# Token rounds of a two-layer Flamingo kernel: router logits computed transposed, routing sums kept in PSUM, one wait for the four quantised tiles

## The reference, cut to what matters

```python
x = x + tanh(g_xattn[0]) * _L0_xattn_ref(ctx, _layernorm(x), conv_w, conv_b, ...)   # adds layernorm(x) and a small convolution
x = x + tanh(g_ffn[0])   * _L0_ffn_ref(_layernorm(x), weight, bias)                 # see below
x = x + tanh(g_xattn[1]) * _L1_xattn_ref(_layernorm(x), mask0, ctx, mask1, ctx, U_w, D_param)  # 77 keys per batch
x = x + tanh(g_ffn[1])   * _L1_ffn_ref(_layernorm(x), Wr, W1, W2)                   # 8 experts, top 1

# _L0_ffn_ref: blocks of 32 along the 512 features are scaled to 7.5 and rounded to a 6-bit grid, then
xd = (xq * xs[..., None]).reshape(x2.shape); out = xd @ wd.T + bias

# _L1_ffn_ref
probs = softmax(t @ Wr, axis=-1); idx = argmax(probs); pmax = max(probs)   # Wr is 512 x 8
onehot = one_hot(idx, 8); pos = sum(cumsum(onehot, axis=0) * onehot, -1) - 1; kept = pos < cap   # cap = 1280
# tokens that are kept go through relu(t W1[e]) W2[e] and are scaled by pmax; the others keep t
```

## Time and profile before

| | |
|---|---|
| median of three runs | 2079.48 us |
| the profiled execution's own time | 2079.27 us |
| its span, first to last instruction | 2077.6 us |
| PE busy / DVE busy / ACT busy / POOL busy | 1945.7 / 982.1 / 733.9 / 776.7 us |
| mean granted TensorE clock | 0.968 of full speed |

### The profile page before, as it was taken

The page is one execution under the profiler, slowest core; times in us unless marked ns, Lnnn a source line. Parts: engine busy times, 40 slices in busy tenths (PEclk is TensorE's granted clock), DMA queues, the critical chain, the costliest instruction groups (busy, mean ns, idle before and its releaser), DMA issues.

```text
span 2077.6 us, 35395 instructions
## 1 busy us (share of the span) xinstructions
PE 1945.7 (94%) x11276; PEld 1681.7 (81%) x11277; DVE 982.1 (47%) x2270; ACT 733.9 (35%) x1691; POOL 776.7 (37%) x803
## 2 busy tenths in 40 slices
PE   4589999999999939999999999999999999999997
PEld 2568787787788728989889998999898898899986
DVE  3678999999998472333311142114224124112331
ACT  2235656656656442332411142114214114211231
POOL 0556576676674232342411142114305115211250
PEclk9589999999999959999999999999999999999999
DMA  6221343353343464341510043004305104300220
GB/s 198 98 88 43 138 174 120 130 172 117 138 163 102 162 209 123 97 142 42 168 42 30 30 143 94 30 30 141 108 16 180 36 30 154 95 30 30 75 87 11
DMA packets 152270, 208.81 MB, mean 101 GB/s; under 512 B 12830, under 2 KB 78622, under 8 KB 152197
## 3 DMA queue, kind: packets, MB, share of 16 engines
q1 hardware_dynamic: 111125, 114.14, 17.4%
q0 software_dynamic: 15728, 43.38, 6.9%
q10 hardware_dynamic: 25344, 50.33, 6.7%
HBM read 140.98 MB, written 68.37 MB: 101 GB/s over the span
## 4 chain that ended last, share of the span: by engine, by line
PE 82%; DVE 7%; issue 3%; DVEq 1%; ACT 1%; POOL 1%; POOLq 0%; ACTq 0%
PE bank L785 24%; PE bank L793 23%; PE bank L1469 9%; PE bank L1398 7%; PE bank L733 6%; PE bank L753 6%; PE bank L1450 2%; DVE x2T_lo L1788 1%; PE bank L711 1%; PE bank L742 1%; PE bank L1406 1%; DVE lg L1903 1%; DVE xdT_lo L1788 1%; DVE lb L1900 1%; DVE rd L1913 0%
## 5 line engine op out<-in xcount | busy, mean ns | idle before, releaser
L893 DVE SCALAR_TENSOR_TENSOR hT_lo<-bank,hT_hi 128x256 fp32r<-128x256 f32 x352 | 149.3, 424 | 671.4 <-ACT hT_hi L661 669.6
L661 ACT ACTIVATE hT_hi<-bank 128x256 fp32r<-128x256 f32 x352 | 135.1, 384 | 748.3 <-PE bank L785 733.5
L785 PE MATMUL bank<-inT_hi,w_lo 128*128 128x256 f32 x1408 | 398.5, 283 | 0.0
L785 PE MATMUL bank<-inT_lo,w_hi 128*128 128x256 f32 x1408 | 398.3, 283 | 0.0
L785 PE MATMUL bank<-inT_hi,w_hi 128*128 128x256 f32 x1408 | 396.9, 282 | 0.6 <-DVEq L941 0.6
L785 PEld LDWEIGHTS bank<-inT_hi,w_hi 128*128 128x128 f32 x1408 | 269.0, 191 | 14.3 <-DVEq L941 1.0
L793 PE MATMUL bank<-w_hi,hT_hi 128*128 128x512 f32 x704 | 279.9, 398 | 0.0
L785 PEld LDWEIGHTS bank<-inT_lo,w_hi 128*128 128x128 f32 x1408 | 269.0, 191 | 12.0
L793 PE MATMUL bank<-w_lo,hT_hi 128*128 128x512 f32 x704 | 277.7, 394 | 0.0
L793 PE MATMUL bank<-w_hi,hT_lo 128*128 128x512 f32 x704 | 274.1, 389 | 0.0
L785 PEld LDWEIGHTS bank<-inT_hi,w_lo 128*128 128x128 f32 x1408 | 269.0, 191 | 0.0
(11 more groups left out here) (312 smaller groups left out, 4019.2 us busy)
## 6 DMA issues: line engine op xcount, KB each, us to landing
stage<-in_L_ffn_W_dram SPq DMA_DIRECT2D x256, 256.0 KB, 3.1
X<-in_x_dram SPq DMA_DIRECT2D x16, 1024.0 KB, 5.3
t_d<-tt ACTq DMA_DIRECT2D x16, 1024.0 KB
x_d<-x ACTq DMA_DIRECT2D x16, 1024.0 KB
out_dram<-y ACTq DMA_DIRECT2D x16, 1024.0 KB, 8.4
xs<-in_x_dram SPq DMA_DIRECT2D x16, 768.0 KB
cw_a<-in_L_xattn_conv_w_dram SPq DMA_DIRECT2D x2, 1024.0 KB, 17.5
cw_b<-in_L_xattn_conv_w_dram SPq DMA_DIRECT2D x2, 1024.0 KB, 19.7
```

What stands on the lines that cost most here:

```text
L661: act.activation(hT_hi[:, f % 4, :], hb[f % 4][:, 0:CN], ACT.Relu).then_inc(e_hh, 1)
L785: last = pe.matmul(hb[f % 4][:, 0:CN], l[:, k, fs], r[:, k, :], start=(n == 0), stop=(n == 3 * KB - 1))
L893: dve.scalar_tensor_tensor(out=hT_lo[:, f % 4, :], in0=hb[f % 4][:, 0:CN], scalar=0.0, in1=hT_hi[:, f % 4, :].bitcast(F32), op0=ALU.max, o ...
```

## The change

The matmuls of `linear`, `project` and `attend` keep their order. What changes:

1. `logits(k)` now has the 16 columns of `wr_hl` as stationary operand and streams all 512 tokens of the group: eight matmuls per step in place of 32, a pair after each three matmuls of `project(1)`, into 16 partitions of bank 1 (`p_lT`).
2. ScalarE copies those 16 x 512 logits to SBUF (`lT`), between `rstd_of_squares("c")` and `up(2)`, and TensorE turns them back with four small transposes into `q_la` (`turn_logits`, after `project(2)`).
3. The routing sums: `q_lb` times `scf` is written to a joint buffer `lq`, a reduction over four parts gives `lg`, and a copy brings the next step's `q_la` into `lq`. `lg`, `rw` and `rd` lie in PSUM (bank 5). One instruction of the chain goes. `scaled_logits`, which reads `rd`, moves ahead of `alT_lo`.
4. GpSimd waits once for all four quantised tiles ahead of its four dequantising products.

```diff
@@ GpSimd, body
                 if a is not None:
+
+                    wait(pool, v_q, T * (a + 1))
+                    settled(pool)
                     for j in range(T):
-
-                        wait(pool, v_q, T * a + j + 1)
-                        settled(pool)
                         pool.tensor_tensor(n1[:, j, :]...
@@ ScalarE, body
                     if j == 0:
                         wait(act, p_cu, KB * b)
-                        wait(act, p_la, b)
+                        wait(act, p_lt, b)
...
                     rstd_of_squares("c", b, sq_c, a_sq, rs_c[:, ds((b % T) * T, T)])
+                if c is not None:
+                    wait(act, p_lt, c + 1)
+                    wait(act, p_la, c)
+                    act.activation(lT[:, :], p_lT, ACT.Copy).then_inc(a_lt, 1)
                 up(2)
@@ TensorE, body
-                def logits(j):
-                    if j == 0:
-                        wait(pe, v_la, c)
-                    js = slice(j * P, j * P + P)
-                    for k in range(KB):
-                        for part in (x2T_hi, x2T_lo):
-                            last = pe.matmul(q_la[:, j, :], part[:, k, js], wr_hl[:, k, :], start=(k == 0 and part is x2T_hi),
-                                             stop=(k == KB - 1 and part is x2T_lo), skip_group_check=True)
-                    if j == T - 1:
-                        last.then_inc(p_la, 1)
+                def logits(k):
+                    if k == 0 and b is not None:
+                        wait(pe, v_x2, T * b + 3)
+                    for part in (x2T_hi, x2T_lo):
+                        last = pe.matmul(p_lT, wr_hl[:, k, :], part[:, k, :], start=(k == 0 and part is x2T_hi),
+                                         stop=(k == KB - 1 and part is x2T_lo))
+                    if k == KB - 1:
+                        last.then_inc(p_lt, 1)
+
+                def turn_logits():
+                    if c is None:
+                        return
+                    wait(pe, a_lt, c + 1)
+                    wait(pe, v_la, c)
+                    for j in range(T):
+                        last = pe.transpose(q_la[:, j, :], lT[:, j * P:j * P + P], ident[0:2 * E, 0:2 * E])
+                    last.then_inc(p_la, 1)
...
                 project(2)
+                turn_logits()
                 turn_quantised(0)
@@ VectorE, body
                 if a is not None:
                     shift("b", a)
+                if not final(d):
+                    scaled_logits()
                 if d is not None:
                     wait(dve, a_th, d + 1)
                     dve.tensor_tensor(alT_lo...
...
-                    dve.tensor_reduce(lb[:, :, :], two_parts(q_lb), AX.X, ALU.add).then_inc(v_r, 1)
-                    dve.tensor_tensor(lb[:, :, :], lb[:, :, :], per_expert(scf), ALU.mult).then_inc(v_r, 1)
-                    dve.tensor_tensor(lg[:, :, :], lb[:, :, :], la[:, :, :], ALU.add).then_inc(v_r, 1)
+                    dve.tensor_tensor(parts_at(0), q_lb[:, :, :], per_expert(scf, 2 * E), ALU.mult).then_inc(v_r, 1)
+                    dve.tensor_reduce(lg[:, :, :], lq[:, :, :, :].rearrange("p j w e -> p j e w"), AX.X,
+                                      ALU.add).then_inc(v_r, 1)
...
-                    dve.tensor_reduce(la[:, :, :], two_parts(q_la), AX.X, ALU.add).then_inc(v_la, 1)
+                    dve.tensor_copy(parts_at(2), q_la[:, :, :]).then_inc(v_la, 1)
```

More of the change, by code:

```diff
@@ L143, in flamingo_two_layers @@
         wr_hl, cwr = tb("wr_hl", [P, KB, 2 * E], F32R), tb("cwr", [L, B, 2 * E], F32R)
-        la = small("la", T, E)
         sum_c, nm_c, sq_c, rs_c = small("sum_c", T), small("nm_c", T), small("sq_c", T), small("rs_c", T * T)
@@ L148, in flamingo_two_layers @@
         smx, nbx, ssm, srd, scf = (small(n, T) for n in ("smx", "nbx", "ssm", "srd", "scf"))
-        rmx, rd, re_, rsum, rp = small("rmx", T), small("rd", T, E), small("re_", T, E), small("rsum", T), small("rp", T)
-        rw, rwm, oh, ohb = small("rw", T, E), small("rwm", T), small("oh", T, E), small("ohb", T, E, dt=BF16)
+        rmx, rsc, re_, rsum, rp = small("rmx", T), small("rsc", T, E), small("re_", T, E), small("rsum", T), small("rp", T)
+        rwm, oh, ohb = small("rwm", T), small("oh", T, E), small("ohb", T, E, dt=BF16)
         cntb = small("cntb", E, dt=BF16)
@@ L155, in flamingo_two_layers @@
         pay = small("pay", T, 2)
-        inputs_end, smalls_end = 2 * KB * CN * 4, smalls_size[0]
-        assert smalls_end >= inputs_end
+        inputs_end = 2 * KB * CN * 4
+        tb("smalls_room", [P, inputs_end // 4 + 2 * NC - smalls_size[0] // 4], F32)
+        assert smalls_size[0] == inputs_end + 2 * NC * 4
         with nc.sbuf_tensor("stage", [P, RING, 2, D], F32) as stage:
@@ L179, in flamingo_two_layers @@
         g_u, g_x1, g_xb, g_xd, g_y = (sem("g_" + n) for n in ("u", "x1", "xb", "xd", "y"))
-        a_n1, a_bh, a_sq, a_ch, a_uh, a_st, a_al, a_th, a_tt, a_sd, a_re, a_mc, a_md = (
-            sem("a_" + n) for n in ("n1", "bh", "sq", "ch", "uh", "st", "al", "th", "tt", "sd", "re", "mc", "md"))
-        p_bt, p_bm, p_ct, p_cu, p_cs, p_cr, p_ca, p_co, p_la, p_lb, p_dp = (
-            sem("p_" + n) for n in ("bt", "bm", "ct", "cu", "cs", "cr", "ca", "co", "la", "lb", "dp"))
+        a_n1, a_bh, a_sq, a_ch, a_uh, a_st, a_al, a_th, a_tt, a_sd, a_re, a_mc, a_md, a_lt = (
+            sem("a_" + n) for n in ("n1", "bh", "sq", "ch", "uh", "st", "al", "th", "tt", "sd", "re", "mc", "md", "lt"))
+        p_bt, p_bm, p_ct, p_cu, p_cs, p_cr, p_ca, p_co, p_la, p_lb, p_dp, p_lt = (
+            sem("p_" + n) for n in ("bt", "bm", "ct", "cu", "cs", "cr", "ca", "co", "la", "lb", "dp", "lt"))
         v_ln = {k: sem(f"v_ln_{k}") for k in "ab"}
@@ L194, in flamingo_two_layers @@
         l_banks = q_banks = bank[1], bank[2]
+        p_lT = bank[1][0:2 * E, :]
         u_banks = bank[3], bank[0]
@@ L326, in flamingo_two_layers @@
         alT_lo = tb("alT_lo", [L, G], F32R)
-        lb, lg, rsc = (small(n, T, E) for n in ("lb", "lg", "rsc"))
+        lT = tb("lT", [2 * E, G], F32)
+        lq = small("lq", T, 4, E)
         def convolved(eng):
@@ L1428, in attend @@
                         if d > 0:
-                            wait(pe, v_r, 8 * (d - 1) + 1)
+                            wait(pe, v_r, 7 * (d - 1) + 1)
                     if j >= 2:
@@ L1732, in scaled_logits @@
                     wait(dve, a_rs["d"], 2 * (e + 1))
-                    wait(dve, v_r, 8 * e + 5)
+                    wait(dve, v_r, 7 * e + 4)
                     dve.tensor_tensor(rsc[:, :, :], rd[:, :, :], per_expert(rs_d), ALU.mult).then_inc(v_re, 1)
@@ L1818, in body @@
                     dve.tensor_scalar(scf[:, :], srd[:, :], gx[:, ds(d, 1)], None, ALU.mult).then_inc(v_scf, 1)
-                if not final(d):
-                    scaled_logits()
-                    if not final(e):
-                        scale_of_y()
+                if not final(d) and not final(e):
+                    scale_of_y()
                 if final(c):
@@ L1906, in body @@
                     if d is not None:
-                        wait(dve, v_r, 8 * d + 3)
-                    dve.tensor_reduce(la[:, :, :], two_parts(q_la), AX.X, ALU.add).then_inc(v_la, 1)
+                        wait(dve, v_r, 7 * d + 2)
+                    dve.tensor_copy(parts_at(2), q_la[:, :, :]).then_inc(v_la, 1)
                 if d is not None:
-                    wait(dve, v_r, 8 * d + 3)
+                    wait(dve, v_r, 7 * d + 2)
                     dve.tensor_reduce(rmx[:, :], lg[:, :, :], AX.X, ALU.max).then_inc(v_r, 1)
-                    wait(dve, v_r, 8 * d + 4)
+                    wait(dve, v_r, 7 * d + 3)
                     dve.tensor_tensor(rd[:, :, :], lg[:, :, :], per_expert(rmx), ALU.subtract).then_inc(v_r, 1)
-                    wait(dve, v_r, 8 * d + 5)
+                    wait(dve, v_r, 7 * d + 4)
                     dve.scalar_tensor_tensor(out=rw[:, :, :], in0=rd[:, :, :], scalar=0.0, in1=rev[:, :, :],
                                              op0=ALU.is_equal, op1=ALU.mult).then_inc(v_r, 1)
-                    wait(dve, v_r, 8 * d + 6)
+                    wait(dve, v_r, 7 * d + 5)
                     dve.tensor_reduce(rwm[:, :], rw[:, :, :], AX.X, ALU.max).then_inc(v_r, 1)
-                    wait(dve, v_r, 8 * d + 7)
+                    wait(dve, v_r, 7 * d + 6)
                     dve.tensor_tensor(oh[:, :, :], rw[:, :, :], per_expert(rwm), ALU.is_equal).then_inc(v_oh, 1)
@@ L1926, in body @@
                     dve.tensor_reduce(ohs[:, :], oh[:, :, :].rearrange("p j e -> p e j"), AX.X, ALU.add).then_inc(v_r, 1)
-                    wait(dve, v_r, 8 * d + 8)
+                    wait(dve, v_r, 7 * d + 7)
                     wait(dve, v_oh, 3 * d + 2)
```

10 lines of the change are left out of this document (5 added, 5 removed).

## The result

The changed kernel takes 2064.49 us (median of four, 2063.22 to 2067.11) against 2079.68 us before in the same comparison: ratio 0.9925 (95% interval 0.9913 to 0.9937), 15.2 us faster where 30 were forecast, 0.5 us outside the range. The spans are 2063.5 and 2077.6 us, a gain of 14.1.

| | forecast | measured |
|---|---|---|
| ten full steps | 10 x 2.2 = 22 | 10 x 1.51 = 15.1 |
| filling and draining steps | 6 x 1.4 = 8.4 | 4.7 |
| expert part, not touched | 0 | -5.7 |
| sum | 30.4 | 14.1 |

What follows compares the result with a forecast made beforehand. Full steps were taken as bound by TensorE's own stream, 38.68 us, with two small holes. Logits 16 x 1.4 = 22.4, stalls 10 x 0.8 = 8, +1 and -1 elsewhere: 30.4 us off, 2049 us, range 2044 to 2056.

Steps and rivals of the forecast that it cites:

- the some 1300 us of experts move as a block: Expert part after the token rounds: nothing in it is touched, so it only starts sooner, with 0 us of change.
- Logits, 1.4 us a step: TensorE's `project(1)`: eight matmuls replace 32, 1.67 us less, minus 0.27 for turning back; 16 x 1.4 = 22.4 us.
- Routing sums, 2.4 us off VectorE: VectorE's `lb`, `lg`, `rd`: with operands in PSUM they no longer wait for GpSimd, 2.4 us less.
- Stalls, 0.8 us a step: TensorE's holes before `al` and `attend(0)`: 0.8 us gained a step of a possible 1.25, in ten steps 8 us.
- The two terms that I had bounded and left small: VectorE's tail: two-input instructions each losing a GpSimd instruction; casts `cntb`, `ohb` each costing up to 1.26 us.
- The single wait: "no wait", +1 in filling steps: GpSimd's wait for four quantised tiles: TensorE does not wait; filling steps gain as `q8` end 1.7 us sooner, +1 with draining.
- 6 x 1.4 = 8.4 with "+1 together, with -1": Six filling and draining steps: logits gain 1.4 us each; +1 from `q8` and draining, -1 for a new hole.
- A: No new hole: GpSimd's lateness is hidden and both old TensorE holes close, 36.9 us gained, 2042; chance 0.17.
- C: Slower: GpSimd's lock all along VectorE's tail brings `al` 3.6 us later, +14 us, 2093; chance 0.04.
- D: Matmuls with 16 stationary columns cost 0.40 us, so only the stalls' 8 us are won, 2071; chance 0.03.
- B: GpSimd's lock makes VectorE late again, each full step losing 0.5 us: 17.4 us gained, 2062; chance 0.14.
- The hole that I forecast ahead of the fourth `turn_second`: TensorE's fourth `turn_second` waits for VectorE's late `up_lo` of tile 3: a new hole of 0.5 us.

Runs made afterwards that it cites:

- b_addr: Kernel before with tile `la` moved so that everything behind the small tiles, experts' tiles included, lies 128 bytes lower: 2083.1 us, ratio 1.0024.
- a_addr: Changed kernel with 128 bytes of padding, putting the tiles behind the small ones back where they lay before: 2060.2 us, ratio 0.9916.
- b_logits: Kernel before with only the new logits matmuls, the copy to `lT` and the turning back: 2072.0 us, ratio 0.9968.
- b_sums: Changed kernel with the old logits and four separate GpSimd waits, so only the routing sums are new: 2070.5 us, ratio 0.9963.
- a_am: Changed kernel with `a_m` in PSUM from step 2 on: 2058.2 us, ratio 0.9897.
- a_counts_later: Changed kernel with `cntb`, `ohb`, `ohs` and `counts` moved behind the next step's `nbx`: 2061.4 us, ratio 0.9923.
- b_one_wait: Kernel before with only GpSimd's single wait for all four quantised tiles: 2084.3 us, ratio 1.002.
- after: The changed kernel as made, against the kernel before: 2064.5 us, ratio 0.9925.
- a_own_waits: Changed kernel with GpSimd's four separate waits for the quantised tiles back: 2059.6 us, ratio 0.9899.

## Why the prediction was wrong

**"After them nothing is touched: the some 1300 us of experts move as a block."** This failed: 5.7 of the 16.3 us that were missing. (The full steps are short by 6.9, the filling and draining ones by 3.7.) The code was not touched, but its tiles were moved by 128 bytes. b_addr and a_addr show it from both sides. The diff said so, in the tiles it adds and drops; I read it for instructions alone.

**Logits, 1.4 us a step.** The price was right: 4.70 us forecast as 4.69, turning 0.35 us as 0.27, so 1.3 us off TensorE. The failed step is "all 16 groups pass this stage, on TensorE's path each time". In full steps VectorE's stream was about as long as TensorE's; b_logits gives 0.1 to 0.2 a step there. I had written that both streams start from `project(3)` and took that to mean that an earlier start shortens both. It moves VectorE's start only if VectorE is waiting, and its timeline had hardly any idle time, 0.64 us before one `up_lo` the longest that I had read.

**Routing sums, 2.4 us off VectorE.** Right as far as the sums themselves go (`rd` 0.20 us; the reduction over four parts 0.41 rather than some 0.2). b_sums shows that these, and not the logits, give the full steps most of their gain: 1.3 us.

**Stalls, 0.8 us a step.** Measured 0.2 (1.5 less the logits' 1.3). The two terms that I had bounded and left small decided it. `a_sc` lost most of a GpSimd instruction (0.95 us; freeing it, and with it mostly `cntb`, gave the step 0.8, a_am), and so did `cntb` and `counts` (0.34 us reached the step, a_counts_later). Of the cast I had said that no row showed one blocked for long, and left it out; no row before the change had one beside GpSimd's adds. The Trainium skill (VectorE: DVE Perf Modes, section "Mode 2x_2P") says that such a copy uses both read ports, and the row of `cntb`, 1269 ns at the median, agrees with it. The trace of the kernel before did hold a warning that I overlooked, an instruction with a single SBUF input that was held as well:

```profile
408.69 0.47 DVE L1663 TENSOR_SCALAR over<-pos 128x4 f32<-128x4 f32 x1
```

It ends at 409.16, and GpSimd's running instruction (the third of y) at 409.14; with GpSimd silent `over` takes 0.16. So the condition "two SBUF inputs" was too narrow, and a row said so. The prediction's other rule from the Trainium skill (VectorE: DVE Perf Modes, section on the TRN2 errata), the dearer PSUM source, does not show here: `rd`'s successor takes 0.20 us in PSUM beside 0.192 for `oh` in the earlier trace rows.

**The single wait: "no wait", +1 in filling steps.** Wrong in sign. That the four `q8` end 1.7 us sooner is so, but the first dequantised tile comes later by more, and TensorE needs the first before the last. b_one_wait puts the price at 4.8 us, part of it in full steps. The forecast that GpSimd would come late relative to TensorE and block `a_m` and `a_sc` was right, and that is this part's doing: with four waits `a_sc` is free.

**The filling and draining steps, 6 x 1.4 = 8.4 with "+1 together, with -1".** They gave 4.7. The single wait costs 1.7 + 0.6 us in the first two (after against a_own_waits; a_am shows that one such step can differ by 1.6 without it), and the copy to `lT`, which I had covered with 3.7 us of work, had no such cover in the step where ScalarE also splits weights: 2.3 us. Together 4.6, a little more than the 3.7 missing. This sum is rough: the 0.8 us of the longer step counts on the same side, and the clock's part, some 3 us, on the other. The experiments do not settle this row to better than a few us.

**Rivals.** A (no new hole) and C (slower) did not come. D is refuted by the spacing of the matmuls. B named the right mechanism and the nearest time, 2062. But it had the step gaining 0.9 us, where it gained 1.5, and it knew nothing of the experts or of the clock; that its time is close is in part a cancellation, and so luck. The hole that I forecast ahead of the fourth `turn_second` did not appear as such; the lost time showed as the hole before `attend(0)` that I had closed.

**Still open.** Why 32 bytes more or less change the spacing of the experts' matmuls, and which of the moved tiles matters: all of them were moved together. Paddings above 128 bytes were not tried. The steps of b_logits alternate in their hole before `al`; why it gained 0.1 to 0.2 and not 0.4 a step, as its listed waits would give, is not settled. Nor is what brings the single stretches of half clock inside full steps: b_addr, whose instructions are those of the kernel before, has one at 345.5 us in a step of 40.1.

## What to carry to other kernels

Before costing a change to one engine, lay the streams of all engines over one period: where two are nearly the same length, cutting one buys little in the steady state, and the same cut is worth more beside a cut of the other (the logits 0.1 alone, 0.5 with the sums). Where VectorE's two-input instructions or casts, all of them on SBUF, fall among GpSimd's, each can be held until the instruction that GpSimd is in is over; a change that moves either stream moves these waits, so check every such instruction behind the change, and give one input a place in PSUM where it lands on the path. When a diff adds or drops a tile, note which addresses shift, and time the unchanged part apart. Compare the granted clock of the two traces stage by stage before giving a gain to the code.

## What the hardware showed that I had not expected

- The experts' stretch, with the same 6336 matmuls of 256 and 512 columns in it, takes 1242.0 to 1259.6 us, 1.4%, by the position of the tiles alone, moved in steps of 32 bytes, and between two positions the difference was spread over the whole stretch.
- A cast of 128 x 8 from SBUF to SBUF took 1.27 us when it started just after a boundary of GpSimd's adds, and 0.16 us when moved (a_counts_later). A two-input instruction with one input in PSUM is not held: `a_sc` 1.11 us and 0.16 us.
- A shorter total of GpSimd's work can be worse. Its dequantising fell from 5.23 to 4.06 us a step, and the single wait that this needed cost the kernel 4.8 us (b_one_wait).
- Executions of one kernel spread with their mean granted clock: the kernel before took 2074.9 to 2075.7 us at 0.971 and 2083.3 to 2084.0 at 0.965.
